# Attention and two layer norms on one core: the first three rounds in new orders

## The chip, the core and the metric

The kernel runs on one core of a Trainium2 chip. TensorE (PE) multiplies, VectorE (DVE), ScalarE (ACT) and GpSimd (POOL) do the element work, and SyncE (SP) and ACT issue DMAs. The metric is the device time of one execution in microseconds. A profiled execution gives the span of the trace, and its own device time beside it.

## The reference

Input x has 8 batches of 2048 tokens with 512 features (E). Two blocks stand one behind the other, each normed, and added to its input behind another layer norm:

```python
x = x + _layernorm(_L0_attn_ref(_layernorm(x, axis=-1), Wq, bq, Wk, bk, Wv, bv, Wo, bo), axis=-1)
x = x + _layernorm(_L0_ffn_ref(_layernorm(x, axis=-1), ..., ln_g, ln_b), axis=-1)

# _L0_attn_ref, h = 16 heads, d = 32
def proj(W, b):
    y = jnp.einsum('nse,fe->nsf', x, W) + b
    return y.reshape(n, s, h, d).transpose(0, 2, 1, 3)
scores = jnp.einsum('nqhd,nkhd->nhqk', Q, K) * scale
attn = jax.nn.softmax(scores, axis=-1)
out = jnp.einsum('nhql,nlhd->nqhd', attn, V).reshape(n, s, e)
return jnp.einsum('nse,fe->nsf', out, Wo) + bo

# _L0_ffn_ref: cap = s_len // n_head
yn = (y - mu) * jax.lax.rsqrt(var + 1e-05) * ln_g + ln_b      # y = t + outs
```

The einsum's letters fall on the transposed axes, so the scores of one token are 16 by 16, head against head, and the softmax runs over 16 values. In the second block the first axis is 8 long, so `cap` is 8 // 16 = 0, no token is chosen, `outs` is zero, and what is left is a layer norm with `ln_g` and `ln_b`.

## The kernel before, in words

The 16384 tokens are 128 tiles of 128 tokens, t = 0 to 127, in 64 pairs v = t // 2. Everything is written out by hand, engine by engine, and every dependence is a semaphore; no planner and no scheduler moves anything. So each engine's order of work is the order of the lines in its block, and an instruction that waits holds up all behind it on its engine.

Numbers in fp32 are split into a high and a low fp16 half. A projection (`project`, L1294, called by `keys`, `queries` and `values`) is twelve matmuls of 128x512: four with x high and W high, four with x high and W low, four with x low and W high.

A pair of x comes twice: as rows (`x_in`, loaded by `load_x` and `next_x`) for its mean and variance (`x_moments` on DVE, `x_root` on POOL), and turned (`x_t`, loaded by `load_xt` and `next_xt`). The statistics go to DRAM and come back spread over all partitions (`rows_store`, L277, and `rows_load`, L283, into `mr_row`). POOL then subtracts and scales (`x_centre` L444, `x_norm` L451), ACT makes the high half (`x_high` L1071), POOL the low half (`x_low` L457). A pair's rows are needed by `x_centre`, that by `x_norm`, `x_high`, `x_low`, and `keys` waits for `xlo_done`.

Keys are turned on DVE (`k_turn` L707) and moved to `k_bd` by four DMAs of SP (`keys_out` L299). Queries pass ACT (`q_in` L1099) and DVE (`q_turn` L714). Values pass ACT (`v_in` L1106), are stored to DRAM from ACT's queue (L1111) and fetched back by SP (`values_back` L321). `scores` (L1357) needs `k_bd`; DVE, ACT and POOL make probabilities of it (`less_top`, `exponent`, `weigh`, `normalise` L513), DVE turns them (`p_turn` L761), and DMAs put them in `p_bd` (`probs_half_out`, half from SP, L310, half from ACT, L1160; from round 2 on `probs_out` of ACT, L1132). `mixed` (L1379) needs `p_bd` and the values, `output` (L1401 to L1405) the output weight.

The four weights are prepared on the chip in the first rounds. For k, q and v, PE spreads the weight's first row over the partitions of a PSUM bank (`spread` L1430), and DVE subtracts that from the weight, half by half (`even_out` L696). ACT sums the squares (`squares` L1090), PE totals them (`totals` L1424), DVE makes a power of two of the total (`scale` L680), ACT casts the scaled weight (`cast` L1081), and DVE makes the low half (`low` L700). The order is k, q, v, o. The row for k and that for v use the same bank, `ps_v`, so PE's second use waits until both halves of k are evened (`w_even` 2).

What is written ahead of the loop `for p in range(2, NV - 1)` on each engine covers pairs 0 and 1 (tiles 0 to 3). I call its two pairs rounds 0 and 1, and the passes of the loop rounds 2, 3 and so on: round p has scores(2p-2) and (2p-1), keys, queries and values of tiles 2p and 2p+1, and the output of two earlier tiles.

## Time and profile before

| | us |
|---|---|
| median of 3 runs | 1566.44 (1565.5 to 1567.25) |
| profiled execution, its own time | 1567.45 |
| its span | 1565.7 |
| PE busy in the span | 1528.8 (98%) |
| DVE busy | 1371.3 (88%) |
| POOL busy | 1356.3 (87%) |
| ACT busy | 839.7 (54%) |

Busy times overlap. PE's time is nearly the span, so the first question is where PE is not busy. The span ends at the last event of the trace; 1.75 us of the execution lie around it.

### The profile page before, as it was taken

To read this page: it belongs to the slowest core of one execution; us is meant where nothing else is said; L and a number is where in the kernel's file an instruction comes from. 1 tells how busy PE (TensorE), PEld (TensorE's weight loads), DVE (VectorE), ACT (ScalarE), POOL (GpSimd) and SP (SyncE) were. 2 spreads that over 40 slices of the span, in tenths; PEclk is the share of its full clock that TensorE was granted. 3 is DMA by queue.
4 is the path that set the end of the run, shared out by engine and by line. 5 is a ranking of instruction groups with operands and counts; after the bars stand their busy time and mean duration, and the time that the engine had idled before them with its cause. 6 is when DMAs were issued, how large, how long until landed. Compare 5 with 4: busy or idle time off the path is not lost.

```text
span 1565.7 us, 59257 instructions
## 1 busy us (share of the span) xinstructions
PE 1528.8 (98%) x22566; PEld 773.4 (49%) x22566; DVE 1371.3 (88%) x2476; ACT 839.7 (54%) x1754; POOL 1356.3 (87%) x1422
## 2 busy tenths in 40 slices
PE   7999999999999999999999999999999999999993
PEld 3445455455554554554554554554554554554541
DVE  7788988988988988988988889888889888888888
ACT  5445465465465565555554554554554554554654
POOL 3668988988988988988988989989989989889867
PEclk9999999999999999999999999999999999999997
DMA  6776766766766766766767767767767767767652
GB/s 235 196 173 162 215 171 191 212 167 195 212 165 198 211 168 198 210 166 202 206 166 206 203 166 208 201 167 210 199 166 212 196 168 213 193 169 214 163 138 95
DMA packets 388651, 293.71 MB, mean 188 GB/s; under 512 B 296854, under 2 KB 296854, under 8 KB 388380
## 3 DMA queue, kind: packets, MB, share of 16 engines
q1 hardware_dynamic: 345936, 223.54, 53.8%
q10 hardware_dynamic: 42444, 66.37, 13.6%
q8 instruction: 192, 3.15, 0.8%
q14 instruction: 79, 0.65, 0.2%
HBM read 155.46 MB, written 67.24 MB: 142 GB/s over the span
## 4 chain that ended last, share of the span: by engine, by line
PE 92%; DVE 3%; POOL 2%; DMA 1%; ACT 1%; issue 1%; SPq 0%; ACTq 0%; POOLq 0%; DVEq 0%
PE ps_k L1299 7%; PE ps_q L1299 7%; PE ps_v L1299 7%; PE ps_v L1300 7%; PE ps_y L1402 7%; PE ps_q L1300 7%; PE ps_k L1300 7%; PE ps_q L1302 7%; PE ps_y L1405 7%; PE ps_y L1401 7%; PE ps_k L1302 7%; PE ps_v L1302 7%; PE ps_s L1357 6%; PE ps_o L1379 5%; DMA x_t<-in_xt 0%
## 5 line engine op out<-in xcount | busy, mean ns | idle before, releaser
L1099 ACT ACTIVATE q_sb<-ps_q,qk_back 128x512 f32<-128x512 f32 x127 | 87.2, 687 | 411.3 <-PE ps_q L1302 400.4
L474 POOL TENSOR_TENSOR o_sb<-o_sb,x 128x512 f32<-128x512 f32 x122 | 153.6, 1280 | 90.6 <-ACT o_sb L1058 90.5
L444 POOL TENSOR_TENSOR x_t<-x_t,mr_row 128x512 f32<-128x512 f32 x126 | 194.4, 1543 | 19.9 <-DMA mr_row<-x_d 10.2
L451 POOL TENSOR_TENSOR x_t<-x_t,mr_row 128x512 f32<-128x512 f32 x126 | 194.8, 1546 | 0.5
L1401 PE MATMUL ps_y<-wo_hi,oT_hi 128*128 128x512 f16 x500 | 190.5, 381 | 0.0
L1402 PE MATMUL ps_y<-wo_lo,oT_hi 128*128 128x512 f16 x500 | 190.4, 381 | 0.0
L1299 PE MATMUL ps_k<-wk_hi,xT_hi 128*128 128x512 f16 x496 | 188.6, 380 | 0.0
L1299 PE MATMUL ps_v<-wv_hi,xT_hi 128*128 128x512 f16 x496 | 188.2, 379 | 0.0
L1300 PE MATMUL ps_v<-wv_lo,xT_hi 128*128 128x512 f16 x496 | 188.2, 379 | 0.0
L1299 PE MATMUL ps_q<-wq_hi,xT_hi 128*128 128x512 f16 x496 | 188.0, 379 | 0.1
L1300 PE MATMUL ps_k<-wk_lo,xT_hi 128*128 128x512 f16 x496 | 188.0, 379 | 0.0
L1300 PE MATMUL ps_q<-wq_lo,xT_hi 128*128 128x512 f16 x496 | 188.0, 379 | 0.0
L462 POOL TENSOR_TENSOR x<-x,res 128x512 f32<-128x512 f32 x124 | 158.0, 1274 | 0.8 <-ACT x L1058 0.8
L457 POOL TENSOR_TENSOR xT_lo<-x_t,xT_hi 128x512 f16<-128x512 f32 x127 | 147.9, 1164 | 11.1 <-ACT xT_hi L1071 11.1
L714 DVE STREAM_TRANSPOSE qT<-q_sb 128x512 f32<-128x512 f32 x128 | 134.3, 1049 | 25.8 <-ACT q_sb L1099 25.8
L468 POOL TENSOR_TENSOR z<-z,b_row 128x512 f32<-128x512 f32 x122 | 155.0, 1271 | 0.0
L725 DVE SCALAR_TENSOR_TENSOR x<-ps_y,y_back,bo_row 128x512 f32<-128x512 f32 x125 | 92.7, 741 | 67.9 <-PE ps_y L1405 67.7
L1106 ACT ACTIVATE v_tok<-ps_v 128x512 f32<-128x512 f32 x127 | 74.4, 586 | 121.1 <-PE ps_v L1302 116.0
L707 DVE STREAM_TRANSPOSE kT<-ps_k 128x512 f32<-128x512 f32 x127 | 131.7, 1037 | 6.8 <-PE ps_k L1318 4.5
L513 POOL TENSOR_TENSOR probs<-probs,inv 128x512 f32<-128x512 f32 x128 | 133.3, 1063 | 4.3 <-DVE inv L754 3.5
L790 DVE TENSOR_TENSOR z<-z,g_row 128x512 f32<-128x512 f32 x120 | 114.9, 996 | 23.8 <-ACT z L1058 23.8
L1405 PE MATMUL ps_y<-wo_hi,oT_lo 128*128 128x512 f16 x500 | 128.3, 379 | 0.0
(226 smaller groups left out, 3355.1 us busy)
## 6 DMA issues: line engine op xcount, KB each, us to landing
x_in<-in_xa SPq DMA_DIRECT2D x64, 512.0 KB, 6.4
...
k_bd<-kT SPq DMA_DIRECT2D x512, 64.0 KB, 3.3
v_d<-v_tok ACTq DMA_DIRECT2D x128, 256.0 KB, 2.5
v_key<-v_d SPq DMA_DIRECT2D x128, 256.0 KB, 4.3
...
p_bd<-pT ACTq DMA_DIRECT2D x500, 64.0 KB, 2.7
...
```

What stands on the lines that cost most here:

```text
L444: nc.gpsimd.tensor_tensor(x_t[v % 2][:, j, :, :], x_t[v % 2][:, j, :, :], mr_row[v % 2][:, :, 0, j].unsqueeze(1).to_broadcast([P, EC, P]), ...
L451: nc.gpsimd.tensor_tensor(x_t[v % 2][:, j, :, :], x_t[v % 2][:, j, :, :], mr_row[v % 2][:, :, 1, j].unsqueeze(1).to_broadcast([P, EC, P]), ...
L457: nc.gpsimd.tensor_tensor(xT_lo[t % 2][:, :, :], x_t[t // 2 % 2][:, t % 2, :, :], xT_hi[t % 2][:, :, :], ALU.subtract).then_inc(xlo_done, 1)
L462: nc.gpsimd.tensor_tensor(x1[:, v % 3, j, :], x1[:, v % 3, j, :], res[:, v % 2, j, :], ALU.add).then_inc(x1_done, 1)
L468: nc.gpsimd.tensor_tensor(z[:, v % 2, j, :], z[:, v % 2, j, :], b_row[:, :], ALU.add).then_inc(z_done, 1)
L474: nc.gpsimd.tensor_tensor(o_sb[:, v % 2, j, :], o_sb[:, v % 2, j, :], x1[:, v % 3, j, :], ALU.add).then_inc(out_done, 1)
L1299: nc.tensor.matmul(ps, x_hi[:, e, :], w_hi[:, e, :], start=e == 0, stop=False)
L1300: nc.tensor.matmul(ps, x_hi[:, e, :], w_lo[:, e, :], start=False, stop=False)
L1302: mm = nc.tensor.matmul(ps, x_lo[:, e, :], w_hi[:, e, :], start=False, stop=e == EC - 1)
L1401: nc.tensor.matmul(to, o_hi[:, a, :], wo_hi[:, a, :], start=a == 0, stop=False)
L1402: nc.tensor.matmul(to, o_hi[:, a, :], wo_lo[:, a, :], start=False, stop=False)
L1405: mm = nc.tensor.matmul(to, o_lo[:, a, :], wo_hi[:, a, :], start=False, stop=a == EC - 1)
```

## The change

No arithmetic is added or dropped. Orders change on SP, DVE, ACT and PE, one bank is another one, and two waits are placed elsewhere. POOL's order stays. Lines of the kernel after are two or three off from those of the kernel before.

```diff
-        w0_bank = {"k": ps_v[:, :], "q": ps_q[:, :], "v": ps_v[:, :]}
+        w0_bank = {"k": ps_v[:, :], "q": ps_q[:, :], "v": ps_o[:, 1, :]}
 SP, behind keys_out(1):
+            next_x(4)
+            sp.wait_ge(w_split, 4)
+            load_r(0)
             values_back(0)
+            keys_out(2)
             values_back(1)
             rows_of(2)
-            keys_out(2)
+            next_xt(3)
             probs_half_out(0)
             probs_half_out(1)
             keys_out(3)
-            next_xt(3)
-            rows_of(3)
-            sp.wait_ge(w_split, 4)
+            rows_store(3)
 SP, in round 2, behind values_back(2) and values_back(3):
-                    next_x(4)
-                    load_r(0)
+                    rows_load(3)
+                if p == 3:
                     load_r(1)
 DVE:
             first_norm(1)
+            dve.wait_ge(xhi_done, 1)
+            (low half of tile 0, L900 of before)
             scale("k")
...
             scale("q")
             product_scale(qk_back, "k", "q", 1.0 / XS ** 2, qk_done)
+            even_out("v", 0)
+            low("q", 0, wq_hi, wq_lo)
             even_out("v", 1)
-            low("q", 0, wq_hi, wq_lo)
             low("q", 1, wq_hi, wq_lo)
...
             low("v", 0, wv_hi, wv_lo)
+            low("v", 1, wv_hi, wv_lo)
             k_turn(1)
-            low("v", 1, wv_hi, wv_lo)
...
+            weigh(0)
+            weigh(1)
+            p_turn(0)
+            q_turn(2)
+            p_turn(1)
+            k_turn(3)
             scale("o")
             product_scale(y_back, "v", "o", 1.0, y_scale_done)
-            weigh(0)
-            weigh(1)
-            q_turn(2)
-            p_turn(0)
-            p_turn(1)
-            k_turn(3)
             x_moments(3)
             q_turn(3)
+            low("o", 0, wo_hi, wo_lo)      (was in round 2)
+            low("o", 1, wo_hi, wo_lo)      (was in round 2)
 ACT:
             probs_half_out(0)
+            probs_half_out(1)
             v_in(2)
-            probs_half_out(1)
+            cast("o", 0, wo_hi)
             q_in(3)
+            cast("o", 1, wo_hi)            (was in round 2)
             x_high(4)
-            cast("o", 0, wo_hi)
 PE, project() for tiles 0 and 1: x high by W high, then x low by W high, then x high by W low
 (before: W low second). queries(1) waits for w_even 6, which values(0) did before.
-            pe.wait_ge(w_even, 2)
             spread("v")
```

**DVE in rounds 0 and 1.** First the rows of before from the second half of q to the low half of q; `o_sb` is the raw v weight, `res` the raw q weight.

```order
L696 TENSOR_TENSOR o_sb<-o_sb,ps_v 128x1024 [waits wv_loaded0,w0_spread]
L680 TENSOR_SCALAR w_exp<-ps_s 128x1 [waits w_total]
L683 TENSOR_SCALAR w_scale<-w_exp 128x1 [waits w_power]
L685 TENSOR_SCALAR w_back<-w_exp 128x1
L690 SCALAR_TENSOR_TENSOR qk_back<-w_back 128x1 [waits w_scaled]
L696 TENSOR_TENSOR o_sb<-o_sb,ps_v 128x1024 [waits wv_loaded1,w0_spread]
L700 SCALAR_TENSOR_TENSOR wq_lo<-res,w_scale,wq_hi 128x1024 [waits w_cast] x2
L707 STREAM_TRANSPOSE kT<-ps_k 128x16x32 [waits k_ready]
```

The same place on DVE in the kernel after:

```order
L682 TENSOR_SCALAR w_exp<-ps_s 128x1 [waits w_total]
L685 TENSOR_SCALAR w_scale<-w_exp 128x1 [waits w_power]
L687 TENSOR_SCALAR w_back<-w_exp 128x1
L692 SCALAR_TENSOR_TENSOR qk_back<-w_back 128x1 [waits w_scaled]
L698 TENSOR_TENSOR o_sb<-o_sb,ps_o 128x1024 [waits wv_loaded0,w0_spread]
L702 SCALAR_TENSOR_TENSOR wq_lo<-res,w_scale,wq_hi 128x1024 [waits w_cast]
L698 TENSOR_TENSOR o_sb<-o_sb,ps_o 128x1024 [waits wv_loaded1,w0_spread]
L702 SCALAR_TENSOR_TENSOR wq_lo<-res,w_scale,wq_hi 128x1024 [waits w_cast]
L709 STREAM_TRANSPOSE kT<-ps_k 128x16x32 [waits k_ready]
```

The first half of v has moved from ahead of q's scale to behind it, and the two halves of v now alternate with the two low halves of q.

**SP in rounds 1 and 2.** One piece of the difference, from `keys_out(1)` on; `mr_row<-x_d` is `rows_load`, `x_d<-mr` is `rows_store`, `v_key<-v_d` is `values_back`.

```order
+L262 DMA x_in<-in_xa 128x1024 [waits stats_doneX]
+L268 DMA res<-in_xr 128x1024 [waits w_split]
 L321 DMA v_key<-v_d 128x16x32 [waits v_stored0]
+L299 DMA k_bd<-kT 32x512 [waits s_ready,kT_done]
+L299 DMA k_bd<-kT 32x512 x3
 L321 DMA v_key<-v_d 128x16x32 [waits v_stored1]
 L277 DMA x_d<-mr 128x4 [waits root_doneX]
 L283 DMA mr_row<-x_d 128x512 [waits mr_stored0]
-L299 DMA k_bd<-kT 32x512 [waits s_ready,kT_done]
-L299 DMA k_bd<-kT 32x512 x3
+L265 DMA x_t<-in_xt 128x1024 [waits xlo_done]
```

Two loads of 512 KB stand ahead of the values' return, and keys 2 between the two returns, so `rows_load(2)` has more in front of it and pair 3's x behind it. Farther down `rows_load(3)` stands behind the returns of tiles 2 and 3 instead of ahead of them.

**ACT in round 1.** One piece of the difference, behind the first half of tile 0's probabilities.

```order
-L1106 ACTIVATE v_tok<-ps_v 128x512 [waits v_stored0,v_ready]
-L1111 DMA v_d<-v_tok 128x512 [waits v_moved0,vtok_done]
 L1160 DMA p_bd<-pT 32x512 [waits p_zeroed,pT_done]
 L1160 DMA p_bd<-pT 32x512
-L1099 ACTIVATE q_sb<-ps_q,qk_back 128x512 [waits qT_done,q_ready]
-L1067 COPY x_t<-lead 1x128 [waits centred]
-L1071 ACTIVATE xT_hi<-x_t 128x512 [waits v_ready,dev_put]
+L1106 ACTIVATE v_tok<-ps_v 128x512 [waits v_stored0,v_ready]
+L1111 DMA v_d<-v_tok 128x512 [waits v_moved0,vtok_done]
```

The probabilities of tile 1 go out ahead of the values of tile 2.

## Rows read from the trace of the kernel before

**Rows 1.** Windows view: us, busy us and count by engine, PEclk, DMA.
```profile
500.00:1000.00 500.00, 500.00 (x7415) 253.15 (x7414) 445.38 (x808) 270.82 (x572) 450.34 (x469) 1.00 0.70 191
```
**Rows 2.** Waits view, PE, 0 to 90 us: who waited for whom.
```profile
PE ps_k L1308 <- ACT wk_hi L1081: 1.7, 1, 1.7
PE ps_o L1379 <- issue: 0.8, 1, 0.8
PE ps_s L1357 <- DMA k_bd<-kT: 0.8, 1, 0.8
```
**Rows 3.** Timeline of PE, rounds 0 and 1: start, length, instruction.
```profile
11.00 2.07 PE L1430 MATMUL ps_v<-v_key,ones 1*128 1x512 f32 x2 [0.64 <-DVE x L696]
12.99 1.01 PE L1424 MATMUL ps_s<-w_sq,one_col 128*128 128x1 f32 x4
...
19.71 1.79 PE L1318 MATMUL ps_k<-wk_hi,xT_lo 128*128 128x512 f16 x4 [0.30 <-DVE xT_lo L900]
...
27.91 1.03 PE L1318 MATMUL ps_q<-wq_hi,xT_lo 128*128 128x512 f16 x4
...
38.27 1.04 PE L1308 MATMUL ps_k<-wk_hi,xT_hi 128*128 128x512 f16 x4
```
**Rows 4.** Timeline of DVE, same stretch.
```profile
22.18 1.19 DVE L696 TENSOR_TENSOR o_sb<-o_sb,ps_v 128x1024 f32<-128x1024 f32 x1
23.29 0.15 DVE L680 TENSOR_SCALAR w_exp<-ps_s 128x1 int32<-128x1 int32 x1
...
24.94 2.47 DVE L700 SCALAR_TENSOR_TENSOR wq_lo<-res,w_scale,wq_hi 128x1024 f16<-128x1024 f32 x2
```
**Rows 5.** Timeline of PE around round 2 and the start of round 3.
```profile
57.66 0.85 PE L1379 MATMUL ps_o<-p_bd,v_key 64*32 64x64 f32 x64 [0.98 <-DMA p_bd<-pT]
...
59.77 0.39 PE L1299 MATMUL ps_k<-wk_hi,xT_hi 128*128 128x512 f16 x1
...
80.59 0.86 PE L1357 MATMUL ps_s<-k_bd,qT 64*32 64x64 f32 x64
82.21 0.85 PE L1357 MATMUL ps_s<-k_bd,qT 64*32 64x64 f32 x64 [0.77 <-DMA k_bd<-kT]
...
85.33 0.39 PE L1299 MATMUL ps_k<-wk_hi,xT_hi 128*128 128x512 f16 x1
```
**Rows 6.** Timeline of SP's queue, rounds 1 and 2: start and length of the issue.
```profile
44.40 1.59 SPq L277 DMA_DIRECT2D x_d<-mr  x1
47.69 0.33 SPq L283 DMA_DIRECT2D mr_row<-x_d  x1
...
60.88 0.32 SPq L283 DMA_DIRECT2D mr_row<-x_d  x1
...
75.70 2.71 SPq L299 DMA_DIRECT2D k_bd<-kT  x4
```
**Rows 7.** Landing of the value store (L1111) issued at 38.7 us.
```profile
DMA to landing us min/median/max: 2.0/2.0/2.0
```
**Rows 8.** Landing of the value store (L1111) issued at 68.4 us.
```profile
DMA to landing us min/median/max: 6.2/6.2/6.2
```
**Rows 9.** Timeline of POOL, rounds 1 and 2.
```profile
51.87 1.53 POOL L444 TENSOR_TENSOR x_t<-x_t,mr_row 128x512 f32<-128x512 f32 x1 [2.16 <-DMA mr_row<-x_d]
...
56.07 1.15 POOL L457 TENSOR_TENSOR xT_lo<-x_t,xT_hi 128x512 f16<-128x512 f32 x1
...
65.41 1.53 POOL L444 TENSOR_TENSOR x_t<-x_t,mr_row 128x512 f32<-128x512 f32 x1 [2.69 <-DMA mr_row<-x_d]
67.02 2.40 POOL L451 TENSOR_TENSOR x_t<-x_t,mr_row 128x512 f32<-128x512 f32 x1
69.54 1.06 POOL L513 TENSOR_TENSOR probs<-probs,inv 128x512 f32<-128x512 f32 x1
```
**Rows 10.** Landing of keys (L299) issued in 26 to 40 us.
```profile
DMA to landing us min/median/max: 2.0/2.3/3.5
```
**Rows 11.** Landing of keys (L299) issued in 74 to 85 us.
```profile
DMA to landing us min/median/max: 4.3/4.7/5.2
```

More of the change, by code:

```diff
@@ L920, in _ @@
             less_top(1)
+            weigh(0)
[4 more added lines that the diff above has]
+            k_turn(3)
             scale("o")
             product_scale(y_back, "v", "o", 1.0, y_scale_done)
-            weigh(0)
-            weigh(1)
-            q_turn(2)
-            p_turn(0)
-            p_turn(1)
-            k_turn(3)
             x_moments(3)
             q_turn(3)
+            low("o", 0, wo_hi, wo_lo)
+            low("o", 1, wo_hi, wo_lo)
             for p in range(2, NV - 1):
@@ L941, in _ @@
                 o_low(b - 4)
-                if p == 2:
-                    low("o", 0, wo_hi, wo_lo)
                 k_turn(a)
-                if p == 2:
-                    low("o", 1, wo_hi, wo_lo)
                 weigh(a - 2)
@@ L1219, in _ @@
             probs_half_out(0)
+            probs_half_out(1)
             v_in(2)
-            probs_half_out(1)
+            cast("o", 0, wo_hi)
             q_in(3)
+            cast("o", 1, wo_hi)
             x_high(4)
-            cast("o", 0, wo_hi)
             o_high(0)
@@ L1237, in _ @@
                 exponent(b - 2)
-                if p == 2:
-                    cast("o", 1, wo_hi)
                 if pair(v):
@@ L1308, in project @@
                     nc.tensor.matmul(ps, x_hi[:, e, :], w_hi[:, e, :], start=e == 0, stop=False)
-                for e in range(EC):
-                    if t == 0 and e % 2 == 0:
-                        pe.wait_ge(w_split, 2 * n + e // 2 + 1)
-                    nc.tensor.matmul(ps, x_hi[:, e, :], w_lo[:, e, :], start=False, stop=False)
-                if t == 0:
-                    pe.wait_ge(first_low, 1)
-                elif k == "k" and t in (2, 3):
-                    pe.wait_ge(xlo_done, t)
-                for e in range(EC):
-                    mm = nc.tensor.matmul(ps, x_lo[:, e, :], w_hi[:, e, :], start=False, stop=e == EC - 1)
+                if t in (2, 3):
+                    for e in range(EC):
+                        nc.tensor.matmul(ps, x_hi[:, e, :], w_lo[:, e, :], start=False, stop=False)
+                    if k == "k":
+                        pe.wait_ge(xlo_done, t)
+                elif t == 0:
+                    pe.wait_ge(first_low, 1)
+                for e in range(EC):
+                    mm = nc.tensor.matmul(ps, x_lo[:, e, :], w_hi[:, e, :], start=False, stop=t in (2, 3) and e == EC - 1)
+                if t in (0, 1):
+                    for e in range(EC):
+                        if t == 0 and e % 2 == 0:
+                            pe.wait_ge(w_split, 2 * n + e // 2 + 1)
+                        mm = nc.tensor.matmul(ps, x_hi[:, e, :], w_lo[:, e, :], start=False, stop=e == EC - 1)
                 mm.then_inc(ready, 1)
@@ L1452, in _ @@
             values(0)
-            spare(14)
+            spare(16)
             values(1)
```

10 lines of the change are left out of this document (4 added, 6 removed).

## The prediction

> **What bounds the kernel now.** I read the windows first. From 500 to 1000 us PE is busy for 500.00 of 500.00 us, DVE for 445 and POOL for 450 [rows 1]: in the loop PE is the bound, the others have a tenth to spare. The change leaves PE's instructions in the loop alone, so it can gain only where PE idles, or runs slowly, before that state sets in, and it can lose only by a new wait of PE. Then PE's waits up to 90 us [rows 2] and its timeline [rows 3, 5]: the reader is to see that PE's last idle time ends at 84 us, and that keys(6) starts round 3's projections at 85.33 [rows 5]. From there PE never waits. So the question is one number: where will keys(6) start? What it gains there the end gains.
>
> There are two stretches with losses: the weights' preparation, up to keys(2) at 38.27 [rows 3], and rounds 2 and 3, where PE waits 0.98 for the probabilities of tile 1, 0.77 for keys of tile 5, and 0.8 in the middle of a row of small matmuls for nothing that the profile shows [rows 2, 5]. Between the two, and from 59.77 to 80.59, PE runs without a gap: these 20.82 us are eight products of twelve matmuls, and I carry them over.
>
> **Part 1, the value row in another bank.** Its wait of 0.64 goes [rows 3]; behind it stands k's total (12.99), then scale, cast and keys(0). The squares of k are nearly as late, so I take 0.64 and not more. The row's own work, 2.07, is done either way. ps_o's second half is first needed by queries(1), far behind.
>
> **Part 2, weights q and v on DVE.** The low half of tile 0 moves from behind k's low halves into the hole ahead of k's scale, where DVE had waited for PE. With W low last, keys(0) waits no longer 0.30 for it [rows 3]. keys(0) ended at 19.71 + 4 x 0.43 = 21.43 (1.79 for four, overlap included); it should end 0.64 + 0.30 + some 0.2 sooner, at 20.3. The total takes 1.01 (L1424) [rows 3], so scale q starts at 21.3 instead of 23.29, where it had stood behind half of v (22.18) [rows 4]. From there to the end of q's low halves DVE had 23.29 to 24.94 + 2.47 = 27.41, that is 4.1 for the scale, one half of v and two low halves; now there is one half more (1.19): 21.3 + 4.1 + 1.2 = 26.6. Gain 0.8. Then PE had two W-low and four x-low matmuls left (27.91 is the start of the last four), now two W-low ones: four at 1.03 / 4, less overlap 0.215 each, are 0.86. So queries(0) ends 1.7 sooner. Both low halves of v now stand ahead of k_turn(1), which takes a short wait out of values(0); none of the rows has its size, it lies between 0 and one such half (1.2), and I take 0.5, since one half is behind the other by no more than a turn. keys(2) then starts at 38.27 - 2.2 = 36.1.
>
> **Part 3, the probabilities and the first half of round 2.** DVE turns tile 0's and 1's probabilities before the scale of o, and ACT sends tile 1's ahead of values 2. The wait of 0.98 should be gone: PE would be ready for keys(4) at 59.77 - 2.2 - 0.98 = 56.6 [rows 5]. What is late next is keys(4)'s own input, the low half of tile 4. In the trace before, pair 2's rows are sent for at 47.69 and x_centre(4) starts at 51.87, x_low(4) ends at 56.07 + 1.15 = 57.22 [rows 6, 9]: 5.35 from the one to the other, POOL's order being the same. Only an earlier `rows_load(2)` moves that. On SP it now has in front of it two 512 KB loads, keys 2 (four issues, 2.71 in such a row [rows 6]) and the same two returns. The first return waits for the value store of tile 0. A store in a quiet stretch landed after 2.0 us [rows 7], one in the burst of round 2 (five transfers of 512 KB) after 6.2 [rows 8]. The new store comes 2.2 to 2.5 us sooner than before but behind two such transfers. Between 2.0 and 6.2 I take 3.7, two fifths of the way: the return can start about 0.8 sooner. The second return no longer waits for its own store but stands behind keys 2, which costs up to 2.7 and gives back up to 2.7. And the statistics' store behind a return was slow before too (1.59 [rows 6]). So `rows_load(2)` comes at 47 to 48, x_centre(4) at 51 to 52, and keys(4) at 56.6 to 57.6; I take 57.2, a gain of 2.6.
>
> By the Trainium skill (DMA: Bandwidth & Descriptors, Queues, rings and completion order) a transfer's semaphore increment lands only after every earlier write of that DMA engine, on whatever queue. By that rule the value store could not be seen before x and the residual have landed; the two rows 2.0 and 6.2 agree with it. Without any such effect (2.0) the sum would be 1.7 better at `rows_load(2)`, but only 0.6 at keys(4), where PE itself is next.
>
> **Part 4, round 2, where the sum is decided.** DVE no longer makes the low halves of o in round 2 but in its idle time before; SP's burst is smaller by x 4 and both residuals; `rows_load(3)` goes behind the returns of tiles 2 and 3. Before, it was issued at 60.88 and x_centre(6) started 4.53 later, at 65.41 [rows 6, 9]. Now it waits for the value store of tile 3, which ACT sends behind x_high(4) and two o_highs. From x_centre(4) at about 51.5: x_norm ends 3.1 later, and five ACT steps of 0.5 to 0.6 make 57.4; the store lands 2.0 or more later; then the return, and behind a return an issue of 1.6 instead of 0.3. That is 61.5 at the earliest, 63 with 3 us for the store: later than before by 0.6 to 2.1. So x_centre(6) starts at 66 to 67.5; I take 66.5.
>
> From there: x_norm had taken 2.40 beside DVE's low half of o [rows 9]; that half is gone, so 1.53 as x_centre, and normalise(2), 4.13 behind x_centre before (65.41 to 69.54), is 3.25 behind it: 69.75. So POOL, not DVE, decides here, and the 0.9 saved just pays for the later rows. From normalise(2) to the keys of tile 5 on SP it was 6.16 (69.54 to 75.70 [rows 6, 9]); DVE was the later of the two there, by little, so I keep it: 75.9. The fourth key DMA is issued 2.1 later and landed before at about 82.1. In the burst keys took 4.3 to 5.2 to land [rows 11], in a quiet stretch 2.0 to 3.5 [rows 10]. The burst is mostly gone, ACT's probability DMAs are not. Bounds 2.0 and 5.2; I take 3.0, inside the quiet ones: 75.9 + 2.1 + 3.0 = 81.0. scores(5) had started at 82.21. PE itself is ready at 57.2 + 20.82 + 0.7 = 78.7, so it now waits 2.3 there, more than before: most of what rounds 0 and 1 gained is given back. The 0.8 behind it I keep by half, as a DMA jam may be its cause: 0.4.
>
> **Sum.** keys(6) at 85.33 - 1.2 - 0.4 = 83.7, gain 1.6. Profiled execution 1567.45 - 1.6 = 1565.9. It was 1.0 above the median of the runs, so for the median 1566.44 - 1.6 = 1564.8. A difference below 0.2% (3.1 us) is no change that a measurement of this kernel can tell.
>
> **Rivals.**
> 1. *The preparation's gain stays.* If the rows of pair 3 come no later than before (65.4) the wait for keys 5 shrinks: 65.4 + 3.25 + 6.16 + 2.1 + 2.3 = 79.2, scores(5) 3.0 sooner, and with the 0.8 gone 3.8; with PE alone as the bound it is 82.21 - 78.0 + 0.8 = 5.0. For it: DVE and the queue are both lighter in round 2. Against it: the store of tile 3 hangs on x_high(4). Median 1561.4 to 1563.3; I name 1562.3.
> 2. *All taken back.* Keys land as before, 4.3 to 5.2 behind the last issue: 75.9 + 2.1 + 4.3 = 82.3. PE waits 3.6 and keys(6) starts at 85.3: 1566.4.
> 3. *Slower: the rows behind the returns.* The store of tile 3 lands like that at 68.4 us, after 6.2 instead of 3 [rows 8], as x 5 and pair 3's x are near: x_centre(6) at 69.5, keys 5 at 84 to 85.5. From x_centre(6) at about 67.7 on, keys landing at 3.0, it is slower than before; at 69.5 by 2, with keys landing at 4.7 by 3.5: 1568.5 to 1570.
> 4. *The clock.* keys(0) runs at 0.43 per matmul of 512 columns, keys(2) at 0.215 (1.04 for four, overlapping) [rows 3]: the two levels, 1.2 and 2.4 GHz, though the windows print a granted clock of 1.00. PE had then run for most of 11 to 21 us. If it now stays at the lower level through keys(1) and queries(0), 24 x 0.215 = 5.2 are added, of which 1 is hidden by q's low halves; keys(2) would then start at 40.3, 2 later than before. Most of it meets the wait for keys 5. 1567 to 1569. The Trainium skill (TensorE: Matmul & The Clock Gate, Part 1) has the array start slow and speed up by recent activity, at a point that varies between runs; a PE that is busy sooner, as here, would by that rule rise no later, which speaks against this rival.
>
> **Chances.** Forecast (gain 0.5 to 3) 0.48; rival 1 0.30; rival 2 0.12; rival 3 0.07; rival 4 0.03. Faster by over 0.2%: rival 1, and a little of the forecast, 0.31. Slower by over 0.2% (above 1569.6): parts of 3 and 4, 0.05. Within: 0.64. The range for 8 in 10 goes from inside rival 1, 1561.8, to the lower end of rival 3, 1567.6; the forecast's own is 1563.4 to 1566.
>
> **What will show it.** k's total at 12.3; scale q at 21.3; keys(2) at 36.1; no wait for p_bd in mixed(1); keys(4) at 57.2 behind x_low(4); `rows_load(3)` issued at 61.5 to 63 and x_centre(6) at 66 to 67.5; PE waiting 1.5 to 3 for k_bd ahead of scores(5); keys(6) at 83.7; no PE wait from there. The prediction is wrong if keys(6) starts before 82 (rival 1, and Part 4 fails), or if PE waits in round 3 or later, which nothing in the trace lets me expect.

## The result: 0.22% slower, and the profile after

| | before | after |
|---|---|---|
| median, us | 1567.11 (1565.5 to 1568.93, 8 runs) | 1570.78 (1570.25 to 1572.1, 8 runs) |
| ratio, with its 95% interval | | 1.0022 [1.0013, 1.0031] |
| profiled execution, its span | 1567.45, 1565.7 | 1571.48, 1569.8 |
| keys(2), keys(4), keys(6) start | 38.27, 59.77, 85.33 | 35.06, 63.04, 89.14 |

The forecast was 1564.8 with a range up to 1567.6; the kernel came out slower than all of it. It is slower by 3.7 us, and keys(6) starts 3.81 later: as forecast, that one number carries to the end. The prediction was right up to keys(2) and wrong from there.

Windows of the kernel after: us, busy us and count of PE, PEld, DVE, ACT and POOL, PEclk, DMA share, GB/s.

```profile
50.00:60.00 10.00, 4.85 (x154) 3.01 (x152) 3.32 (x3) 2.77 (x6) 5.41 (x6) 0.81 0.57 134
60.00:70.00 10.00, 8.85 (x142) 4.50 (x141) 6.30 (x11) 3.65 (x7) 3.81 (x3) 0.68 0.54 106
500.00:1000.00 500.00, 500.00 (x7415) 252.97 (x7414) 445.91 (x809) 270.08 (x569) 450.50 (x469) 1.00 0.70 193
```

The loop is as it was [rows 1]. In 50 to 60 us PE is busy for less than half, and the granted clock falls to 0.81 and then 0.68. The timeline of PE, where [rows 3, 5] are the rows of before:

```profile
10.24 1.91 PE L1433 MATMUL ps_o<-v_key,ones 1*128 1x512 f32 x2
12.08 1.01 PE L1427 MATMUL ps_s<-w_sq,one_col 128*128 128x1 f32 x4
...
18.29 1.21 PE L1321 MATMUL ps_k<-wk_lo,xT_hi 128*128 128x512 f16 x4
...
35.06 1.03 PE L1307 MATMUL ps_k<-wk_hi,xT_hi 128*128 128x512 f16 x4
...
57.81 2.03 PE L1382 MATMUL ps_o<-p_bd,v_key 64*32 64x64 f32 x127 [5.15 <-issue]
59.53 0.32 PE L1360 MATMUL ps_s<-k_bd,qT 64*32 64x64 f32 x2
59.55 0.31 PE L1382 MATMUL ps_o<-p_bd,v_key 64*32 64x64 f32 x1
59.55 0.49 PE L1360 MATMUL ps_s<-k_bd,qT 64*32 64x64 f32 x11
61.19 1.92 PE L1360 MATMUL ps_s<-k_bd,qT 64*32 64x64 f32 x115 [1.15 <-issue]
63.04 0.61 PE L1298 MATMUL ps_k<-wk_hi,xT_hi 128*128 128x512 f16 x1
...
87.04 0.85 PE L1360 MATMUL ps_s<-k_bd,qT 64*32 64x64 f32 x64 [0.66 <-DMA k_bd<-kT]
```

Up to 52.66 PE is 3.2 us ahead of before. Then it stands for 5.15 us ahead of mixed(0) and for 1.15 within scores, where before it had 0.98 within mixed. The queue of SP, as in [rows 6]:

```profile
34.12 0.58 SPq L262 DMA_DIRECT2D x_in<-in_xa  x1
34.74 0.43 SPq L268 DMA_DIRECT2D res<-in_xr  x1
41.37 0.38 SPq L321 DMA_DIRECT2D v_key<-v_d  x1
41.85 3.08 SPq L299 DMA_DIRECT2D k_bd<-kT  x4
44.98 0.58 SPq L321 DMA_DIRECT2D v_key<-v_d  x1
45.61 1.20 SPq L277 DMA_DIRECT2D x_d<-mr  x1
49.90 0.33 SPq L283 DMA_DIRECT2D mr_row<-x_d  x1
50.28 0.43 SPq L265 DMA_DIRECT2D x_t<-in_xt  x1
50.81 2.41 SPq L310 DMA_DIRECT2D p_bd<-pT  x4
```

The store of tile 0's values leaves at 35.1 and its return can start at 41.37. The view of the two probability DMAs of tile 0 that SP issues (50.8 and 51.4):

```profile
L310 SPq DMA_DIRECT2D p_bd<-pT x2: 513/552/591, 50.8 to 51.4; - x2
...
DMA to landing us min/median/max: 5.6/6.0/6.4
```

51.4 + 6.4 = 57.8, and mixed(0) starts at 57.81. So the wait that the timeline calls "issue" is a wait for `p_bd`. The experiments bear that out seven times more (below). The chain of waits from there (start, length, what):

```profile
52.66 5.15 issue
57.81 2.01 PE ps_o L1382 x120
60.01 0.38 issue
60.39 0.59 ACT oT_hi L1115
60.98 0.50 ACT v_tok L1106
61.50 4.14 DMA v_d<-v_tok
65.65 0.37 SPq L321
66.11 6.22 DMA mr_row<-x_d
72.46 1.55 POOL x_t L446
74.08 1.52 POOL x_t L453
75.60 2.04 POOL probs L515 x2
```

The late mixed(0) makes o_high(1) late, that the value store of tile 3 behind it on ACT, that the return, and that `rows_load(3)`, which the change put behind the return. x_centre(6) starts at 72.46, where [rows 9] had 65.41. After that nothing is lost: the keys of tile 5 leave at 81.34, land in up to 3.5, and PE waits 0.66 for them.

The 3.81 at keys(6) can be added up from PE's rows. keys(4) starts 3.27 later. From there to scores(4) it is 22.48 us (63.04 to 85.52) instead of 20.82, since the first eight matmuls of keys(4) take 3.39 instead of 1.73. From scores(4) to keys(6) it is 3.62 instead of 4.74: waits of 0.77 and 0.80 [rows 2, 5] are gone, and 0.66 is new. So the loss is for the most part PE's own lateness at mixed(0) and the slower matmuls behind it. The chain through pair 3's rows adds about a microsecond, by the trace of e12 (below).

### The profile page after: what moved, and what is told of

Its sections match the earlier page's. It is cut to its first block, busy times and chain, and to the rows that moved or that the text cites. A ratio compares the mean times of both kernels' runs of the same rounds, so it can differ in the third digit from the quotient of the medians.

```text
span 1569.8 us, 59257 instructions
## 1 busy us (share of the span) xinstructions
PE 1530.1 (97%) x22566; PEld 774.6 (49%) x22566; DVE 1370.1 (87%) x2476; ACT 840.1 (54%) x1754; POOL 1354.6 (86%) x1422
## 3 DMA queue, kind: packets, MB, share of 16 engines
q8 instruction: 192, 3.15, 0.8%
## 4 chain that ended last, share of the span: by engine, by line
PE 93%; POOL 3%; DVE 1%; DMA 1%; issue 1%; ACT 1%; SPq 0%; POOLq 0%; ACTq 0%; DVEq 0%
PE ps_k L1298 7%; PE ps_q L1298 7%; PE ps_v L1298 7%; PE ps_v L1299 7%; PE ps_q L1301 7%; PE ps_y L1408 7%; PE ps_y L1404 7%; PE ps_v L1301 7%; PE ps_k L1301 7%; PE ps_y L1405 7%; PE ps_q L1299 7%; PE ps_k L1299 7%; PE ps_s L1360 6%; PE ps_o L1382 5%; DMA mr_row<-x_d 0%
```

## Experiments

Each kernel was timed against the kernel before on its own chip, in several rounds. "rows 2" is the issue of pair 2's rows, x_c(6) the start of x_centre(6). All points in time are of the one profiled execution. That can lie off its kernel's median: e1's is 2.5 us above it and the slowest of its twelve, e5's 2.6 below. So a microsecond at keys(6) between two runs is a hint, and the verdicts go by the ratios. Two ratios, each with 0.0009 either way, are told apart from a difference of about 0.0013 on.

| run | median | ratio [interval] | keys(2) | rows 2 | mixed(0) | keys(4) | x_c(6) | keys(6) |
|---|---|---|---|---|---|---|---|---|
| before | 1567.11 | 1 | 38.27 | 47.69 | 55.82 | 59.77 | 65.41 | 85.33 |
| after | 1570.78 | 1.0022 [1.0013, 1.0031] | 35.06 | 49.90 | 57.81 | 63.04 | 72.46 | 89.14 |
| e1 | 1571.49 | 1.0018 [1.0008, 1.0029] | 35.35 | 52.15 | 56.38 | 61.67 | 72.87 | 90.24 |
| e2 | 1569.63 | 1.0009 [1.0000, 1.0018] | 35.18 | 46.08 | 54.09 | 58.99 | 70.07 | 86.94 |
| e12 | 1570.97 | 1.0014 [1.0006, 1.0023] | 35.28 | 49.61 | 57.73 | 63.26 | 65.28 | 88.06 |
| e13 | 1569.29 | 1.0015 [1.0006, 1.0024] | 36.67 | 48.01 | 57.55 | 62.54 | 71.76 | 88.34 |
| e10 | 1572.06 | 1.0025 [1.0014, 1.0035] | 35.23 | 49.37 | 58.17 | 63.40 | 72.57 | 89.07 |
| e4 | 1564.55 | 0.9974 [0.9965, 0.9983] | 35.30 | 44.21 | 52.84 | 56.34 | 61.75 | 81.78 |
| e16 | 1563.25 | 0.9976 [0.9966, 0.9985] | 35.29 | 44.10 | 52.83 | 56.58 | 60.65 | 80.92 |
| e5 | 1565.30 | 0.9982 [0.9973, 0.9991] | 35.09 | 43.99 | 52.63 | 56.06 | 60.52 | 80.92 |
| e15 | 1564.45 | 0.9981 [0.9973, 0.9990] | 35.02 | 43.85 | 52.56 | 56.00 | 60.90 | 81.96 |
| e6 | 1566.49 | 0.9992 [0.9983, 1.0000] | 35.88 | 46.66 | 53.56 | 59.19 | 64.28 | 84.65 |
| e7 | 1566.10 | 0.9990 [0.9981, 0.9999] | 35.33 | 44.22 | 52.86 | 57.17 | 67.49 | 83.94 |
| e8 | 1565.43 | 0.9985 [0.9976, 0.9994] | 36.02 | 44.86 | 53.56 | 57.99 | 60.65 | 83.74 |
| e14 | 1563.56 | 0.9975 [0.9966, 0.9984] | 35.08 | 45.97 | 52.62 | 56.94 | 61.16 | 81.34 |
| e3 | 1787.95 | 1.1401 [1.1373, 1.1429] | 35.45 | 51.70 | 59.39 | 66.43 | 73.43 | 94.83 |
| e9 | 1576.37 | 1.0051 [1.0038, 1.0064] | 35.09 | 48.67 | 58.34 | 65.93 | 73.34 | 91.62 |
| e11 | 1568.39 | 0.9997 [0.9989, 1.0006] | 38.88 | 48.23 | 56.43 | 60.34 | 65.09 | 86.00 |
| e17 | 1568.92 | 1.0009 [1.0000, 1.0018] | 37.23 | 46.39 | 54.77 | 58.47 | 64.38 | 84.56 |
| e18 | 1566.74 | 0.9992 [0.9983, 1.0001] | 37.50 | 46.78 | 55.05 | 58.58 | 64.33 | 85.46 |

**e4 and e16, the weights' part alone** (Parts 1 and 2 of the prediction; everything else as before):

```diff
 (on the kernel before)
+ value row in ps_o[:, 1, :], no wait for w_even 2 ahead of it; project()'s new order
+ DVE from first_norm(1) to low("v", 1) in the order of after
- spare(14)   + spare(16)      (ahead of values(1))
```

The kernel after has the same `spare(16)`, two NOPs more on PE than before; the diff ahead of the prediction does not show them. The programs before and after have 59257 instructions each.

> The kernel before with the weights' part alone: value row in the other bank, low half of tile 0 ahead of k's scale, halves of v between the low halves of q, both low halves of v together, W low last in the products of tiles 0 and 1. SP, ACT and DVE's order from round 1 on as before. Theory: this part gains 3.2 us up to keys(2) (35.06 in the kernel after, 38.27 before) and brings nothing by itself unless SP's chain follows: values_back(0) at 37.6, rows_load(2) at 44.5, mixed(1) at 54.5 to 55, keys(4) at 56.6. In round 2 all that before had is there, 3 us sooner, so the time is 2 to 3.5 below before. Rival: the low halves of o in round 2 and the big burst of round 2 hold keys 5 at 82.1, so that keys(6) moves by under 1 and the time is that of before.

> The kernel of e4 again (the weights' part alone), beside e15: 0.9965 to 0.9983 of the time before, as in e4.

Faster by 0.24 to 0.26%, twice. Its rows on PE and SP:

```profile
52.84 0.86 PE L1383 MATMUL ps_o<-p_bd,v_key 64*32 64x64 f32 x64
54.27 0.85 PE L1383 MATMUL ps_o<-p_bd,v_key 64*32 64x64 f32 x64 [0.57 <-DMA p_bd<-pT]
```

```profile
37.52 2.95 SPq L321 DMA_DIRECT2D v_key<-v_d  x2
40.51 2.21 SPq L277 DMA_DIRECT2D x_d<-mr  x1
44.21 0.33 SPq L283 DMA_DIRECT2D mr_row<-x_d  x1
```

All of the gain at keys(2) arrives at the end: PE is 3.0 ahead there, 3.4 at keys(4), 3.55 at keys(6). So what the whole change loses, 0.47% against this kernel, lies in the other parts. I put each part of SP's order on this kernel alone, and took each out of the kernel after.

**e5 and e15, the new orders of DVE, ACT and PE, SP's queue as before.**

```diff
 (on the kernel after) SP: its block up to round 2 as in the kernel before
```

> PE, DVE and ACT as after the change; SP's whole order as before it (x 4 and residual 0 in round 2, x^T 3 behind the probabilities, the rows of pair 3 with their load in round 1). Theory A, the loss is all in SP's order: the value store of tile 0 lands in 2 to 3 us, pair 2's rows are sent for at 44 to 45 as in the run with the weights' part alone, the probabilities' DMAs land in 2 to 4, keys(6) starts at 81 to 83, time 1562 to 1565 (2 to 5 below before). Theory B, the new orders of DVE and ACT in rounds 1 and 2 cost as well: they have o's scale and low halves in front of k_turn(4), keys(6) at 85 or later, time 1567 or more. Rival C, the early probabilities on DVE and ACT bring something on top of the weights' part: below 1563.

> The kernel of e5 again (PE, DVE and ACT as after the change, SP's order as before), beside e16 on one chip. If the early probabilities and output weight bring something, it is 0.03 to 0.1% faster than e16, as the one profiled span of each said (1560.9 and 1562.8); if they cost something, 0.03 to 0.1% slower, as the medians of the two chips said (0.9982 and 0.9974 of before); else within 0.03%.

Theory A: with SP's queue as before the 5.15 us are gone, and the ratio goes from 1.0022 to 0.9982 and 0.9981. That is the clearest step of all, so the loss lies in SP's order. The early probabilities and the early output weight bring nothing: the ratio is 0.0005 to 0.0008 above that of the weights' part by itself, which the intervals do not tell from nothing. The wait for tile 1's probabilities (0.57) is gone as meant, and a gap of 0.45 stands within scores instead.

**e6, the early burst, and e2, which takes it out of the kernel after.**

```diff
 e6 (on e4):             e2 (on after):
 keys_out(1)             keys_out(1)
+next_x(4)              -next_x(4)
+sp.wait_ge(w_split,4)  -sp.wait_ge(w_split,4)   (behind rows_store(3))
+load_r(0)              -load_r(0)               (both in round 2, behind rows_load(3))
 values_back(0)          values_back(0)
```

> The kernel with the weights' part alone, and of SP's new order only this: x 4 and residual 0 (two transfers of 512 KB) ahead of the first value's return. Theory A, that burst delays the value store and so the whole chain: value store of tile 0 lands in 5 to 6.5 us instead of about 2, values_back(0) at 41 instead of 37.5, pair 2's rows sent for at 48 instead of 44.2, keys(6) 3 to 4 later than 81.78, time 1567 to 1569. Rival, the burst is hidden by PE's own row of work, as its removal from round 2 gives back there what it takes here: 1563.5 to 1565.5, no difference from the weights' part alone.

> The kernel after, with the loads of x 4 and of the residual of pair 0 (two times 512 KB) taken from ahead of the values' return and put back in round 2, behind rows_load(3); xt 3 stays ahead of the probabilities. Theory Q: the value store of tile 0 lands after 2 to 3 us instead of 6.3, values_back(0) is issued at 37.5 instead of 41.4, rows_load(2) at 45 to 46 instead of 49.9, the probabilities' SP halves at 46 to 48.5; even at 5 to 6 us of landing they are there at 52 to 54, so mixed(0) waits under 1.5 us, keys(4) starts at 55.5 to 57, and keys(6) at 81 to 84: 1 to 4 us below before. Rival: the burst did not matter, SP was held by the statistics' store or the returns themselves; then rows_load(2) stays at 49 to 50 and the time at that of the kernel after, 3.7 above before.

The view of the value store of tile 0, first in e4, then in e6:

```profile
L1111 ACTq DMA_DIRECT2D v_d<-v_tok x1: 367/367/367, 35.3 to 35.3; - x1
...
DMA to landing us min/median/max: 2.2/2.2/2.2
```

```profile
L1111 ACTq DMA_DIRECT2D v_d<-v_tok x1: 373/373/373, 35.9 to 35.9; - x1
...
DMA to landing us min/median/max: 5.4/5.4/5.4
```

The store goes from 2.2 to 5.4, the first return from 37.52 to 41.32 and pair 2's rows from 44.21 to 46.66. The step is as forecast by theory A, the size at the end is smaller: 0.0017 above the mean of e4 and e16, or 2.7 us, and keys(6) 2.9 later than in e4 (I had said 3 to 4, and 1567 at least), of which 0.6 stands there at keys(2) already, ahead of what the edit touches. And the path is another one than I had thought: PE does not wait for data at keys(4) but stands 2.17 within scores, as "issue", and the clock falls behind it (0.91 and 0.92 in 50 to 60 and 60 to 70 us). Taken out of the kernel after (e2), it gives back 0.0013, just at what the intervals can tell. Of e2's forecast the returns, the rows and the wait ahead of mixed(0) (1.31) came as said. But PE stood 1.90 within scores, 1.51 ahead of queries(4) and 2.28 for the keys of tile 5, so keys(6) came at 86.94, not at 81 to 84.

**e10, the burst behind the first return.**

```diff
 (on the kernel after)
 keys_out(1)
+values_back(0)
 next_x(4)
 sp.wait_ge(w_split, 4)
 load_r(0)
-values_back(0)
 keys_out(2)
```

> The kernel after, with x 4 and residual 0 behind the first value's return instead of ahead of it. Theory A, a small store is seen only when the large transfers issued before it have landed: the store of tile 0 lands in 2 to 3 us again and its return is issued at 37.4 instead of 41.4. But two transfers of 512 KB now stand ahead of tile 1's return and of the statistics: pair 2's rows at 47 to 49 (after 49.9), probabilities at 48 to 50, mixed(0) at 55 to 57 (after 57.8), keys(6) 1 to 3 sooner than 89.14, 1568 to 1570.5. Rival, what counts is the share of the DMA engines that the burst takes, wherever it stands: 1570.5 to 1572, as after the change.

The rival held. The store lands in 2.6 and its return leaves at 37.84, but pair 2's rows leave at 49.37 all the same: the keys, tile 1's return (43.34) and the statistics now stand behind the two transfers. So it did not matter on which side of the first return the burst stood.

**e7, pair 3's rows behind the returns, and e12, which takes that out of the kernel after.**

```diff
 e7 (on e4):                    e12 (on after):
-rows_of(3)  +rows_store(3)    -rows_store(3)  +rows_of(3)
+rows_load(3) in round 2       -rows_load(3) in round 2
```

> The kernel with the weights' part alone, and of SP's new order only this: the load of pair 3's rows behind the returns of tiles 2 and 3 in round 2. Theory A, it is on the path: rows_load(3) some 4 us later (57.1 to 61), x_centre(6) from 61.75 to 65 or 66, keys of tile 5 some 3 later, PE waits 1 to 3 ahead of scores(5), keys(6) at 83.5 to 85, time 1566.5 to 1568.5. Rival, PE is the bound there and POOL has slack of that size: 1563.5 to 1565.5, no difference from the weights' part alone.

> The kernel after, with the load of pair 3's rows back in round 1, ahead of the returns of tiles 2 and 3. Theory A, it stood behind a value's store that lands late: rows_load(3) at 57 to 59 instead of 66.11, x_centre(6) no longer last, keys(6) at 86 to 87.5 with PE's wait ahead of mixed(0) unchanged at about 5, 1568 to 1570. Rival, PE alone decides by then, since it had waited only 0.66 for the keys of tile 5: 1570 to 1571.5.

For e7 theory A holds. The rows leave at 61.19 instead of 57.13, and x_centre(6) and the keys of tile 5 follow; SP, POOL and PE of e7:

```profile
54.78 6.31 SPq L321 DMA_DIRECT2D v_key<-v_d  x2
61.19 1.11 SPq L283 DMA_DIRECT2D mr_row<-x_d  x1
```

```profile
67.49 1.53 POOL L445 TENSOR_TENSOR x_t<-x_t,mr_row 128x512 f32<-128x512 f32 x1 [7.35 <-DMA mr_row<-x_d]
```

```profile
81.86 0.85 PE L1362 MATMUL ps_s<-k_bd,qT 64*32 64x64 f32 x64 [1.86 <-DMA k_bd<-kT]
```

These are the late rows of rival 3, at 0.0015 or 2.3 us. In the kernel after they are worth less: e12's difference of 0.0008 is within the intervals, with keys(6) 1.1 sooner. There the rival holds: PE is late itself, and x_centre(6) at 65.28 leaves it without a wait for keys. PE has no idle time at all from keys(4) to keys(6), so 1.16 us of slower matmuls in keys(4) (2.89 for the first eight instead of 1.73) reach keys(6) in full.

**e8, x^T 3 ahead of the probabilities, and e1, which takes that out of the kernel after.**

```diff
 e8 (on e4):              e1 (on after):
 keys_out(2)              rows_of(2)
+next_xt(3)              -next_xt(3)
 probs_half_out(0)        probs_half_out(0)
 ...                      ...
-next_xt(3)               keys_out(3)
 rows_of(3)              +next_xt(3)
```

> The kernel with the weights' part alone, and of SP's new order only this: the transposed x of pair 3 ahead of the SP halves of the probabilities. Theory A, a store issued behind a 512 KB load is seen only when that has landed: the probabilities of tiles 0 and 1 land in 4.5 to 6 us instead of 2 to 3, mixed(0) or mixed(1) waits 1 to 3 us more, and keys(6) is 1 to 3 later than 81.78, time 1565.5 to 1567.5. Rival, the probabilities' landing does not depend on it: 1563.5 to 1565.5, no difference from the weights' part alone.

> The kernel after, with one SP issue put back: pair 3's x (xt 3) goes behind keys_out(3), as before the change. Theory Q (queue): mixed(0) at 57.81 waited for tile 0's and 1's probabilities, whose SP halves were issued at 50.8 to 53.2 behind the 512 KB of xt 3 and took 5.0 to 6.4 us to land instead of 2.0 to 2.6 before. Without xt 3 ahead of them: issued 50.3 to 52.7, landed by 54 to 55.3, so mixed(0) starts at 54 to 54.5, mixed(1) at 55.3. PE then idles for 2 to 3 us instead of 5.15 and should keep its higher clock level (512 columns in 0.215 us in keys(4)). keys(4) starts at 59.8, held by x_low(4). keys(6) at 86, that is 3 us less than the kernel after, 0 to 1 more than before. Rival D (DVE and ACT orders): the wait hangs on something that is late for another reason (values, queries put); then mixed(0) stays at 57.8 and the time stays 3.7 us above before.

In e8 the two DMAs of tile 0 land in 3.7 and 4.0 us, in the kernel before in 2.4 and 2.3. That is less than the 4.5 to 6 forecast, and mixed(0) does not wait for them yet. The ratio is 0.0010 above that of the weights' part, at the edge of what the intervals tell. PE has two "issue" gaps of 1.07 and 1.51, where e4 has one of 0.72; of the 2.0 at keys(6) 0.7 was there at keys(2), ahead of the edit. In the kernel after x^T 3 stands right behind the rows of pair 2, and the landing is longer. In eight kernels the start of mixed(0) is the landing of tile 0's second DMA from SP:

| | issued | landing | sum | mixed(0) | ahead of it on SP |
|---|---|---|---|---|---|
| after | 51.4 | 6.4 | 57.8 | 57.81 | rows, x^T 3 |
| e2 | 47.6 | 6.4 | 54.0 | 54.09 | rows, x^T 3 |
| e9 | 50.1 | 8.1 | 58.2 | 58.34 | rows, x^T 3 |
| e3 | 54.2 | 5.1 | 59.3 | 59.39 | rows, x^T 3 |
| e10 | 50.9 | 7.2 | 58.1 | 58.17 | rows, x^T 3 |
| e12 | 51.2 | 6.5 | 57.7 | 57.73 | rows, x^T 3 |
| e13 | 52.3 | 5.2 | 57.5 | 57.55 | rows, keys 2, x^T 3 |
| e1 | 53.1 | 3.2 | 56.3 | 56.38 | rows |

e1 took x^T 3 away and halved the landing, but its rows left 2.25 later in that execution (its value stores landed in 5.7 to 7.1), so the time is that of the kernel after within the intervals. My expectation of it (keys(6) at 86) failed: it came at 90.24, with a wait of 2.21 for the keys of tile 5. That x^T 3 costs time in the kernel after is not shown; that it lengthens the landing is.

**e13 and e14, the keys of tile 2 between the returns.**

```diff
 e13 (on after):          e14 (on e4):
 values_back(0)           values_back(0)
-keys_out(2)             +keys_out(2)
 values_back(1)           values_back(1)
 rows_of(2)               rows_of(2)
+keys_out(2)             -keys_out(2)
```

> The kernel after, with the keys of tile 2 sent behind pair 2's statistics and rows again, as before the change; the two early transfers, x^T 3 ahead of the probabilities and the late rows of pair 3 stay. Theory A, the four key DMAs cost the rows of pair 2 about 3 us: rows_load(2) at 46.7 instead of 49.90, x_centre(4) at 51.5 instead of 54.33. The probabilities on SP leave at 50.2 to 52, hardly sooner than after the change (50.81), but land in 3 to 4.5 instead of 5 to 6.4 since the rows and x^T 3 no longer leave together: mixed(0) at 55 to 56 instead of 57.81, keys(6) 1.5 to 3 sooner than 89.14, 1568 to 1570. Rival, the keys' place is a draw as the prediction had it: 1570.5 to 1572.

> The kernel with the weights' part alone, and of SP's new order only this: the keys of tile 2 between the two value returns. Theory A: rows_load(2) at 46 instead of 44.21, x_centre(4) at 50.4 instead of 48.56, the rows of pair 3 and the keys of tile 5 some 1 to 2 later, keys(6) 0 to 2 later than 81.78 (PE had no wait for the keys of tile 5 there, so some is hidden), 0 to 0.13% slower than e16. Rival, POOL has slack of that size in round 2: the same as e16 within 0.03%.

By itself it is a draw, as the prediction had it: pair 2's rows leave 1.8 later and x_centre(4) starts at 50.49 instead of 48.56, but pair 3's rows do not (56.91 and 57.13), and the time is that of e16. In the kernel after, the 0.0007 between e13 and it is within the intervals. (In e13's profiled execution all stands 1.6 later from keys(2) on; less that, its rows leave at 46.4 instead of 49.90.)

**e3 and e9, matmuls in the hole ahead of mixed(0).**

```diff
 (on the kernel after)
                 if p == 2:
+                    pe.wait_ge(w_scaled, 7)
+                    for _ in range(26):        (e9: 22)
+                        nc.tensor.matmul(ps_y[:, :], xT_hi[1][:, 0, :], wv_hi[:, 0, :], start=True, stop=True)
                     mixed(0)
 (e9 alone, in round 2)
-                spare(14) four times
+                spare(0), spare(0), spare(0), spare(11)
```

> The kernel after with 26 matmuls of 128x512 added on PE ahead of mixed(0), into a PSUM bank that nothing reads then (26 x 0.215 = 5.6 us, from 52.5 to 58.1). It adds work and computes nothing. Theory C (clock): of the 3.8 us by which the kernel after is late, about 2.6 come from PE running at the lower of its two levels (0.43 per 512 columns) from 57.8 to 66.4 us, because it had idled for 5.15 us. Filled, keys(4) runs at 0.215: mixed(0) starts about 0.3 later (58.1), but keys(6) comes 2 to 2.5 earlier than in the kernel after, and the time is 1 to 1.8 above before. Rival: the level costs nothing, as PE waits later for keys 5 anyway (there it waited 0.66 in the kernel after, so most of the 2.6 would be turned into that wait): then the time stays within 0.5 of the kernel after, and the wait for k_bd ahead of scores(5) grows to 3.

> The kernel after, with 22 matmuls of 128x512 whose result nobody reads ahead of mixed(0), and 45 of round 2's NOPs left out (one for each of the 44 instructions, weight load and matmul, and one for their wait), so that from round 3 on PE's program stands where it stood. It asks two things. The clock: theory A says its fall costs some 2 us at keys(4) (eight matmuls at 0.43 instead of 0.215 each) but nothing at the end, since x_centre(6) and the keys of tile 5 end last: keys(4) at 61 instead of 63.04, keys(6) at 89 as after the change, 1570 to 1572. Rival: the clock is what was lost, 1568 to 1569.5. The NOPs: if a shift of PE's program was the cause of the 40 us in 500 that the run with 26 matmuls and all NOPs idled, that idling is gone, and the gap within scores(0)/(1) stands after about 119 matmuls instead of 13. If it was the matmuls themselves, the time stays near 1788.

e3 was meant to hold the clock and lost 14%: from 500 to 1000 us PE idles 40.4 us, which it does in no other kernel here. Behind 90 us such idle time is 123.5 us in all, of the 215.8 by which its span is longer than that of the kernel after. The rest shows in part as a slower PE: from 500 to 1000 us the granted clock is 0.97, and the first eight matmuls of a keys product are 430 ns long on the mean instead of 379. Waits of PE in that stretch, and the window of e9 for the same stretch:

```profile
PE ps_o L1382 <- issue: 40.4, 18, 2.6
```

```profile
500.00:1000.00 500.00, 500.00 (x7411) 254.04 (x7410) 444.81 (x804) 270.64 (x570) 449.51 (x466) 1.00 0.71 193
```

With 45 NOPs of round 2 left out PE is busy throughout that stretch again, with 22 such matmuls in place. So it was the shift of PE's program. (It is not wholly put back: 44 instructions came and 45 went, see e17.) The gap within scores tells the same; in the kernel after it stands behind 13 matmuls (2 + 11), in e9:

```profile
58.34 1.50 PE L1382 MATMUL ps_o<-p_bd,v_key 64*32 64x64 f32 x128 [0.90 <-issue]
59.64 1.42 PE L1360 MATMUL ps_s<-k_bd,qT 64*32 64x64 f32 x118
65.55 0.44 PE L1360 MATMUL ps_s<-k_bd,qT 64*32 64x64 f32 x10 [4.50 <-issue]
```

22 matmuls more ahead of it, and the gap stands 105 matmuls later: 128 - 22 = 106. In e3, with 26, it is behind 114, and 13 + 128 - 26 = 115. So the gap keeps its place in the program, in steps of 128 matmuls, each a weight load and a matmul. The page counts 192 packets and 3.15 MB on the instruction queue, 16.4 KB each. By the Trainium skill (Runtime: NRT & Kernel Launch, Terms and What's in a NEFF) an engine's instruction memory is refilled in blocks of 16 KiB, and a program is made of instructions of 64 bytes; the packets agree, and 256 such instructions are one. That PE stands there for the next block is inferred: no view shows the fetch itself.

On the clock e9 says nothing: PE idled 4.50 behind the matmuls instead of 5.15 ahead of mixed(0), and the clock fell to 0.67 after all. Its time, 1.0051, is in neither forecast. In the kernel after, what the clock's fall costs at the end stays open; it may be nothing, if PE would only have waited longer for the keys of tile 5. In e12 it is 1.16 at least.

**e11, e17 and e18, Part 1 alone.**

```diff
 (on the kernel before)
+        w0_bank = {..., "v": ps_o[:, 1, :]}      (all three)
-            pe.wait_ge(w_even, 2)                 (e17, e18)
-            spare(14)   +spare(15)                (e18)
```

> The kernel before, with the value row in the other bank and nothing else. Theory A: the wait of 0.64 ahead of the row of v goes, k's total at 12.3 instead of 12.99, keys(2) 0.3 to 0.7 sooner than 38.27, keys(6) 0.3 to 0.7 sooner than 85.33, 1566 to 1567.5 (before on the same chip at about 1567.5), no difference that can be told. Rival, the row is not on the path and keys(2) stays at 38.2. Second rival, the bank is worth the whole of the 0.9 by which k's total came sooner: 1566.3 or less.

> The kernel before, with the value row in the other bank and without PE's wait for the evened k ahead of it; all orders as before. Theory A: the wait of 0.64 goes, k's total at 12.1 to 12.3 instead of 12.99, and keys(0) follows, but then waits 0.9 to 1.2 instead of 0.30 for the low half of tile 0 or for W low, since DVE's order is the old one: keys(2) 0.3 to 0.9 sooner than 38.27, and PE's wait for the probabilities of tile 1 grows by as much, so keys(6) within 0.5 of 85.33, ratio 0.998 to 1.000. Rival, the wait was worth what it lasted to the end: keys(6) 0.6 sooner or more, ratio 0.9975 to 0.999.

> The kernel of e17 with one NOP more on PE in round 0, so that PE's program has the length of before again. Theory A, the place of PE's loop in its instruction stream matters to a single instruction: keys(6) at 84.3 to 84.8 as in e17, no drift from there (e17 drifted by 2.6 us), time 1566 to 1567.3, ratio 0.9985 to 0.9995. Rival, the drift in e17 came by chance or from the bank: 1568 to 1569.5, ratio 1.0003 to 1.0012 as in e17.

e11 kept PE's explicit wait, so the row still waited 0.69 and the run does not test Part 1. Its keys(2) came 0.6 later, since PE stood 1.27 ahead of q's total and ran keys(1) slower behind that (1.77 for four matmuls instead of 1.02, granted clock 0.81 from 21 to 30 us). In e17 the wait is gone, k's total starts at 11.93 and keys(2) at 37.23, a microsecond sooner, and keys(6) 0.8 sooner. But the time went up by 0.09%, which was in neither forecast: the trace loses 2.7 us behind keys(6), bit by bit over the whole loop. Its program has one instruction less than that of before (59256 and 59257 on the page). e18 put a NOP in, and the loop stays within 0.7 us of that of before, at 0.9992. (Its keys(6) came at 85.46 in that execution and not at 84.3 to 84.8: PE stood 1.15 as "issue" ahead of scores(4).) The intervals of e17 and e18 barely overlap, but the traces of all kernels settle it. From keys(6) to the end of the span it is 1479.8 to 1481.9 us in the seventeen kernels of 59257 instructions, and 1483.0 in both that have 59256, e17 and e9. So a single instruction counts, about 2.5 us here.

## Why the prediction was wrong, point by point

- **Parts 1 and 2** held, and gained more than I had worked out: 3.2 at keys(2), not 2.2. k's total came at 12.08 (12.3), scale q at 20.18 (21.3). Two terms were off. PE is at the upper level of its clock sooner: keys(0)'s last four matmuls took 1.21 where [rows 3] has 1.79 (at the upper level four take 1.03). And q's total, for which I had taken k's 1.01, took 0.60. That was a misreading and no gain, for q's own row before the change says the same:

```profile
22.02 0.60 PE L1424 MATMUL ps_s<-w_sq,one_col 128*128 128x1 f32 x4 [0.52 <-ACT wq_hi L1090]
```

Those two are 1.0 of the 1.1 at scale q. Part 1 alone is worth 0.8 to 1.0 at keys(2) (e18, e17), not 0.64; at the end its 0.08% (e18) is not told from nothing. Rival 4, the clock there, went the other way. The rule of the Trainium skill (TensorE: Matmul & The Clock Gate, Part 1) that was cited with it would have it so.
- **Part 3 failed**, and this is where the time went. Its first term, the landing of the value store, was taken as 3.7 between 2.0 and 6.2 [rows 7, 8]; it was 6.3, above the upper bound. The 3.7 was two fifths of the way, for two transfers against five. But of the five only three had been issued when the store left at 68.4, so the bound was that of three, not of five:

```profile
65.08 2.75 SPq L262 DMA_DIRECT2D x_in<-in_xa  x1
67.88 0.90 SPq L268 DMA_DIRECT2D res<-in_xr  x2
68.82 0.43 SPq L262 DMA_DIRECT2D x_in<-in_xa  x1
```

`rows_load(2)` came at 49.90, not at 47 to 48. Of these 2 to 3 us 1.4 is the first return (41.37, where 0.8 ahead of 40.79 was forecast). The rest is mostly the statistics' way, 4.29 from `rows_store(2)` to `rows_load(2)` instead of 3.29 [rows 6]. e6 shows the burst alone to make the rows 2.5 later.
- The larger failure is a term that the sum did not have. It asked when the probabilities leave DVE and ACT, and wrote "the wait of 0.98 should be gone". SP sends half of them, and on SP they stood behind `rows_load(2)` and x^T 3. DVE turned them at 44.4 and 45.9, ACT's half left from 45.15 on and landed in 3.0 to 3.7, but SP issued them at 50.81 and they landed in 5.6 and 6.4. I had moved four issues past two new ones and counted the delay for `rows_load(2)` alone, not for what stands behind it. With both, "no wait for p_bd in mixed(1)" turned into 5.15 ahead of mixed(0).
- **Part 4**: the mechanism was right (the rows behind the return are late, and the value store of tile 3 hangs on o_high), the base was not. `rows_load(3)` at 66.11 is 3 to 4.6 behind the forecast, mostly because mixed(0) was late, and from its issue to x_centre(6) it took 6.35 instead of 4.53 [rows 6, 9] (6.30 in e7, where mixed(0) is not late). It is rival 3, at 72.46 instead of 69.5. But its chance had been 0.07, reckoned on the store's landing alone (4.14 here), and its other terms came cheaper than feared: keys landed in 2.2 to 3.5 behind the last issue (3.0 taken), and PE waited only 0.66, since it was late itself.
- **The gap of 0.8 within a row of small matmuls** [rows 2] I had put down to a DMA jam and counted by half. It is tied to a place in PE's program; it comes to 0.25 to 2.2 in these runs, and to 3.97 and 4.50 in e3 and e9. In round 2 it takes the place of a data wait just ahead: 0.98, 0.57 and 1.37 of waiting within mixed(1) (before, e4, e7) and no gap in scores, no such wait (after, e5, e6, e8, e14) and a gap of 0.45 to 2.17. So a wait of under a microsecond there was not to be had in full. What sets the gap's length is not shown; the kernel after had waited 5.15 ahead of mixed(0) and has the gap all the same.
- The parts add up. Over the weights' part (0.9975): burst 0.0017, pair 3's rows 0.0015, x^T 3 0.0010, keys 2 nothing, DVE and ACT 0.0006, together 1.0023; measured 1.0022. Each difference has an interval of about 0.0013 either way (only the burst and pair 3's rows are clear of it), so the agreement is in good part luck. The burst ahead and the rows behind the returns were bought for round 2, and round 2 had no need of them: in e4 PE's only data wait there is the 0.57 for the probabilities, and none is for keys.
